# Layer 0's attention on TensorE: the next unit's scores moved from a period's fourth slot to its second, behind the values

## What is computed

```python
x = x + L0_xattn(layernorm(x), ctx_1024, ctx_1024, mask, w_q, w_k, w_v, w_o)
x = x + L0_ffn(layernorm(x), ...)          # 64 experts, 8 of them for each token
# in L0_xattn, H = 16 heads of 16 features:
scores = einsum('bhqd,bhkd->bhqk', Q, K) / 4
scores = where(mask == 0, -1e9, scores)
ctx    = einsum('bhqk,bhkd->bhqd', softmax(scores), V)
return ctx @ w_o.T
# in L0_ffn: logits = x @ gate_w, the top 8 of softmax(logits), each token's row goes to the
# buffers of its experts (128 places each), then the experts, and the results are gathered and weighted
```

## Time and profile before

| | before |
|---|---|
| median of 3 runs | 1023.38 us (1022.8 to 1025.14) |
| profiled execution | 1019.77 us, its span 1018.1 us |
| TensorE, matmul | 888.6 us busy, 87% of the span |
| VectorE | 657.3 us, 65% |
| ScalarE | 486.9 us, 48% |
| GpSimd | 539.1 us, 53% |
| mean granted TensorE clock | 0.91 |

### The profile page before, as it was taken

One profiled execution on the slowest core, in us unless ns is written; L12 is line 12 of the kernel. 1 busy time (PEld: TensorE's weight loads), 2 busy tenths in 40 slices (PEclk: granted clock), 3 DMA queues, 4 the chain that ended last, 5 costly groups with the idle time before them and its releaser, 6 DMA issues. The chain is left out here.

```text
span 1018.1 us, 23251 instructions
## 1 busy us (share of the span) xinstructions
PE 888.6 (87%) x6378; PEld 665.7 (65%) x6378; DVE 657.3 (65%) x3249; ACT 486.9 (48%) x1600; POOL 539.1 (53%) x545
## 2 busy tenths in 40 slices
PE   5888888877899999796999999988999999999970
PEld 3566666655479889454676776755788877777740
DVE  2767766764245445345689999867566666666587
ACT  2777667753123333221676676421455555555520
POOL 1006555677424444499806566666555665556630
PEclk9999899986999999997799999659999999999955
DMA  9998511104579993565322222396778554554497
GB/s 323 349 377 305 196 64 64 37 21 174 169 255 319 317 312 125 191 232 207 122 87 86 89 95 98 125 377 253 243 235 267 173 152 150 153 152 138 133 408 238
DMA packets 114449, 198.83 MB, mean 195 GB/s; under 512 B 18840, under 2 KB 86765, under 8 KB 111250
## 3 DMA queue, kind: packets, MB, share of 16 engines
q1 hardware_dynamic: 84210, 138.56, 41.6%
q0 software_dynamic: 23040, 50.38, 13.4%
q10 hardware_dynamic: 7072, 8.40, 2.5%
HBM read 114.01 MB, written 98.98 MB: 209 GB/s over the span
## 5 line engine op out<-in xcount | busy, mean ns | idle before, releaser
L985 POOL DMA_INDIRECT buf<-R,RI x240 | 235.0, 979 | 233.3 <-ACT R L1137 125.3
L770 PE MATMUL PS<-R,XT 128*128 x640 | 155.9, 368 | 5.9 <-DVE XT L1607 5.8
L1021 POOL DMA_INDIRECT yb<-YT,DI x99 | 96.3, 973 | 92.8 <-DVE DI L1600 83.8
L315 PE MATMUL PS<-R 128*128 128x256 f32 (+2 forms) x352 | 117.9, 472 | 16.4 <-DMA R<-in_ctxT 10.2
L1607 DVE COPY XT<-PS 128x256 f32<-128x256 f32 x224 | 94.9, 424 | 45.9 <-PE PS L320 42.7
L770 PEld LDWEIGHTS PS<-R,XT 128*128 128x128 f32 x640 | 107.3, 197 | 14.4 <-issue 7.2
L786 PE MATMUL PS<-R,AT 128*128 (+1 forms) x320 | 102.8, 404 | 0.0
L315 PEld LDWEIGHTS PS<-R 128*128 128x128 f32 (+1 forms) x352 | 69.5, 215 | 48.2 <-issue 32.9
L1137 ACT ACTIVATE R<-R,MX 128x120 f32<-128x120 f32 x256 | 80.1, 387 | 38.2 <-DVE MX L1433 38.1
L1312 ACT ACTIVATE SL<-PS 128x128 f32<-128x128 f32 (+1 forms) x160 | 42.6, 266 | 111.7 <-PE PS L770 110.1
L1137 ACT ACTIVATE R<-PS,MX 128x120 f32<-128x120 f32 x256 | 71.4, 368 | 31.1 <-DVE MX L1433 30.0
(11 more groups left out here) (208 smaller groups left out, 1890.4 us busy)
## 6 DMA issues: line engine op xcount, KB each, us to landing
R<-in_ew SPq DMA_DIRECT2D x64, 384.0 KB, 5.2
BX<-buf SPq DMA_DIRECT2D x128, 140.0 KB
yb<-Z SPq DMA_DIRECT2D x16, 1024.0 KB
R<-yb SPq DMA_DIRECT2D x16, 1024.0 KB, 4.8
R<-buf SPq DMA_DIRECT2D x96, 140.0 KB
R<-in_w SPq DMA_DIRECT2D x8, 1536.0 KB, 11.0
R<-yb SPq DMA_DIRECT2D x8, 1536.0 KB, 10.6
buf<-Z SPq DMA_DIRECT2D x8, 1120.0 KB, 13.3
```

The costliest lines, as they stand in the source:

```text
L315: m = e.matmul(out_, left, right, start=(i == 0), stop=(i == len(pairs) - 1))
L770: x = e.matmul(PS[:, 2 + j % 2, 0:2 * wd], XT[:, j % 3, k, :], src[:, bass.ds(regs[j], 1), k * 2 * wd:(k + 1) * 2 * wd].rearrange("p a n - ...
L985: e.indirect_dma_start(out=(buf1 if l else buf0)[:, :], out_offset=bass.IndirectOffsetOnAxis(ap=RI[:, n % 6, k:k + 1].bitcast(U32), axis=0 ...
L1021: e.indirect_dma_start(out=yb[:, :], out_offset=bass.IndirectOffsetOnAxis(ap=DI[:, j:j + 1].bitcast(U32), axis=0), in_=(YTS0 if i < E0 els ...
```

## The change

In `main` of TensorE the call `scores(u + 1)` of layer 0 moves from slot 3, behind the second transpose, to slot 1, behind the values product of unit u-2 and ahead of the helpers' steps of slots 1 and 2 and of both transposes of unit u-1. Layer 1 keeps its order, and so do all other engines. No instruction is added or removed.

```diff
@@ main(u, slot), TensorE
-                    elif slot == 1 and 0 <= u - 2 < NU:
-                        values(u - 2)
+                    elif slot == 1:
+                        if 0 <= u - 2 < NU:
+                            values(u - 2)
+                        if l == 0 and ahead and u >= 0:
+                            scores(u + 1)
                     elif slot == 2 and 0 <= v < NU:
                         turn(v, 0)
                     elif slot == 3:
                         if 0 <= v < NU:
                             turn(v, 1)
-                        if ahead and (l or u >= 0):
+                        if l and ahead:
                             scores(u + 1)
```

## The result

| | before | changed |
|---|---|---|
| median | 1023.09 us (4 runs, 1022.76 to 1025.14) | 1051.22 us (4 runs, 1049.59 to 1058.24) |
| ratio | | 1.0284, 95% interval 1.0251 to 1.0317 |
| profiled execution | 1019.77 us, span 1018.1 | 1050.04 us, span 1048.4 |
| shared expert begins on TensorE | 249.39 us | 280.21 us |
| granted clock, 22 us to there | 0.90 | 0.77 |

A forecast was written before the change was run, and what follows sets the result against it. The prediction took a ring of waits among TensorE, ScalarE and VectorE, with no owner, to bound layer 0's attention. Delays of 4.1 + 2.5 + 4.4 + 1.5 = 12.5 us on the 1023.4 median gave 1035.9 us, range 1022.5 to 1042.

The forecast's parts named there:

- The sum of the waits: Layer 0's attention: delays of steady periods' queries and rows, first six and last periods, 4.1 + 2.5 + 4.4 + 1.5 = 12.5 us.
- the rows': L1092's copy of turned rows comes later in periods 7 to 23: 0.5 us lost five times, 2.5 us.
- the queries' part: L1099 gets queries later: 0.7 us lost in periods 9, 13, 17, 21 and 1.3 in period 25, 4.1 us.
- The first periods: First six periods, without slack as there is no routing yet: delays in periods 1, 3, 4 and 5, 4.4 us.
- the odd periods as a whole: The sum's terms for odd periods: periods 1, 3, 5, the rows and the queries, 8.9 us together.
- The last periods: Periods 26 to 31, helpers at double pace: only period 28's first transpose is tight, 1.5 us taken.
- The clock: TensorE's granted clock, 0.91 over 22 to 240 us: pauses ahead of L319 stay about as long, neither gain nor loss counted.
- the ring: TensorE, ScalarE and VectorE wait for each other in layer 0's attention: 20.2, 38.1 and 13.6 us, with no owner.
- The third: Rival, faster by the clock: the new rhythm keeps the full clock, at most 15.9 us back, 1020.0 us; chance 8%.
- the fourth: Rival, worse: each of 14 places finds the half clock, 0.85 us more each, 12 us more, 1048; chance 4%.
- The rule weighed: TensorE's score weight loads, idle 4.8 us, could hide better behind another neighbour, giving 1031.1 us; counted as nothing.

The follow-up runs named there:

- fill_after: Changed kernel plus unread spare 128x128 products in TensorE's pauses ahead of L319, even periods 8 to 26; 1027.09 us, ratio 1.0052 against before.
- fill_before: Kernel before, order kept, plus unread spare 128x128 products in TensorE's pauses ahead of L319, even periods 8 to 26; 1011.97 us, ratio 0.9895.
- even_only: Against the kernel before, scores moved to slot 1 in even periods alone, odd periods kept; 1032.56 us against 1021.90, ratio 1.0107.
- even_slot2: Against the kernel before, scores moved in even periods alone to slot 2, behind slot 1's helpers, ahead of the first transpose; 1032.37 us, ratio 1.0114.
- slot2: Changed kernel with scores in slot 2 instead, behind slot 1's helpers, ahead of the first transpose, all periods; 1027.12 us, ratio 1.0049 against before.
- delay_alone_b: Kernel before plus spare ScalarE copies ahead of odd periods' exponentials, 7 to 25; 1036.02 us, ratio 1.0121; without _b, the same on a slow chip, 1.0062.

## Why the forecast was wrong

**The sum of the waits held.** The filled pair ends the attention 13.3 us apart in the profile (15.1 by the medians of fill_after and fill_before, whose intervals are 0.4 and 0.9% wide), 12.5 were summed. Only its middle is free of the clock: 5.0 us over periods 8 to 26, where 6.1 were summed. There both the rows' and the queries' part were a little too big. The first periods with period 7 gave 5.3 against 4.9, and the odd periods as a whole 9.3 us against 8.9. The last periods were sized too small: from the values of period 28 to the end 46.0 us (252.32 - 206.34) against 41.8 (238.96 - 197.19), 4.2 us where 1.5 were taken; but those periods are not filled (0.72 from 206 us on there), so clock is in it, and between 26 and 28 1.2 us came back. The largest part of the 4.2 us is period 30, 7.26 us at a clock of 0.50 against 4.22 at 0.82. That the total of 12.5 came so close is in part luck, as steady terms that were too big and last ones that were too small cancel.

**The step that failed is "The clock": "I count neither gain nor loss".** Its stated reason was that the pauses stay about as long. They are 2.74 us in period 12 and 2.13 in 14 of the changed kernel, where the step said 2.5 and 1.8, and before had 2.56 and 1.61: longer than before in both kinds. Behind it stood an unstated reason, that only pauses count. That one fails too: even_only has the old pauses and still a clock of 0.82 where before has 0.89 over the same part. The term that was put at nothing can be measured over periods 8 to 26, as the filled kernels do the same work there at 1.00. In us:

| | to the values of period 8 | from there to those of period 26 | from there to the shared expert |
|---|---|---|---|
| before | 68.87 | 122.03 | 58.49 |
| changed | 74.75 | 142.13 | 63.33 |
| fill_before | 69.36 | 112.60 | 57.00 |
| fill_after | 74.71 | 117.58 | 60.03 |

The middle windows of before and of the changed kernel:

```profile
68.87:190.90 122.03, 103.07 (x1063) 79.24 (x1062) 85.51 (x339) 83.83 (x288) 66.35 (x68) 0.90 0.46 159
```
```profile
74.75:216.88 142.13, 118.46 (x1064) 91.70 (x1063) 86.39 (x339) 83.64 (x288) 66.51 (x68) 0.77 0.35 120
```

In the middle the clock took 24.6 us in the changed kernel (142.13 - 117.58) and 9.4 us before (122.03 - 112.60). So of the 20.1 us by which the middle got longer, 5.0 are the waits and 15.1 the clock. Of the 30.8 us of the whole attention, 5.9 lie ahead of it and 4.8 behind, and there waits and clock are not told apart.

**Why the loss is so large** is shown by TensorE's stretch from the L319 transpose to the router product. The sum counted it as unchanged, "as the sum ahead of it is the same". At one clock it is: in period 12 4.3 us in fill_before and 4.2 in fill_after. But it lies in the ring, so when it runs at 1.2 GHz its whole stretching is paid: 7.9 us in period 12 of the changed kernel. Over the nine such stretches of periods 8 to 24 it is 55.1 us before and 68.6 changed, and with the spare products 45.4 and 45.0: 9.6 and 23.6 us of stretching, nearly all that the clock took in the middle.

**The rivals.** The third had the mechanism right and the sign wrong. It took the falls of the clock as a reserve that could only come back. They also could grow, and for that side I had only the fourth, which charged the slow clock to the moved scores alone (12 us for 14 places), and not to all that TensorE does in the ring. It came nearest in time, 1048 us against 1051.22, at a chance of 4%. Twelve score groups do run at the half clock in the changed kernel, 1.77 to 1.97 us each, but so do the transposes, the projection and the router product around them. The price of the reserve itself was of the right order: 15.9 us at most, 9.9 measured by filling some of the pauses. The rule weighed, on weight loads, was not put to a test. The idle time with no releaser but issue ahead of the scores' loads went from 4.8 to 3.1 us, so at most 1.7 us came from it.

**What stays open.** Why even_only and even_slot2 spend 71 to 76 us at 1.2 GHz and slot2 56, with pauses of the same length, is not explained. Tested and refused is the neighbourhood of values and scores, as far as one pair of kernels shows it (even_only and even_slot2). The wide spread of even_slot2 (1028.90 to 1040.96) says that the same order can meet the falls differently from one execution to the next; no run tells what sets that. That the pauses are a cause, though not the only one, rests on fill_before, fill_after and delay_alone_b. So it is shown that the clock took the rest of the loss; why this order makes it fall more often is not.

## What to carry to other kernels

When TensorE alternates between its two clocks in a stretch, a sum of waits gives only the part at a fixed clock; price a delay in such a ring at about twice its length (an estimate from two cases: 6 us in, 12 to 13 out for the spare copies; 13.3 in, 30.8 out for this change), and put a falling clock on the slower side of the range, not only on the faster one. Before reordering, try to hold the clock: a few spare products in the pauses that the ring leaves anyway gave 1.0% (ratio 0.9895) and are the best version found here. And when an operation moves ahead of helper steps that another engine's queue waits for in order, charge it to every such step: that part of the working came out within about a microsecond (5.0 us measured at the full clock, 6.1 summed).

## What the runs showed of the hardware

- Spare products of 128x128, 10 and 6 per pause, that left pauses of 0.3 us, held the granted clock at 1.00 over the 112.6 us of periods 8 to 26 (fill_before), where it was 0.90 over the same periods without them.
- The length of the longest pauses alone does not set how much of the time the clock is down. With the same ones ahead of L319 (2.6 us at most), before had 0.89, even_only 0.82 and even_slot2 0.84 from 60 us to the end of the attention, each in one execution.
- One chip ran the kernel before in 1144 us and not 1023. In delay_alone there VectorE's L1454 alone stood 11.1 us with no releaser but issue from 100 to 280 us, and delay_alone_b has no such wait.
